# A tanh recurrence on one Trainium2 core: tanh ahead of the transpose, 32-column matmuls, and a bank and a signal for each output half

## The chip, the cores and the metric

The kernel runs on one core of a Trainium2 chip. The metric is the device time of one execution in microseconds (us), lower is better; the median of several runs is compared. Engines are named as in the profile: PE is TensorE's matmul, PEld its weight load, DVE is VectorE, ACT is ScalarE, POOL is GpSimd, SP is SyncE. Each has an instruction stream of its own, and they meet at semaphores.

## The reference

A block with four layers on x (8 batches, 512 positions, 256 channels). Only the first part is touched by the change, a recurrence over the 512 positions whose every step needs the one before:

```python
xw = jnp.einsum('ntd,dh->nth', x, Wx) + b
def step(prev_h, xw_t):
    next_h = jnp.tanh(xw_t + prev_h @ Wh)
    return (next_h, next_h)
_, hs = jax.lax.scan(step, h0, jnp.swapaxes(xw, 0, 1))
```

Its output goes through a long convolution (decays `exp(-dt*A*t)`), is added to x, and a gated scan and a mixture of 16 experts with a shared one follow. Nothing after the recurrence can begin before its last step.

## The kernel before, in words

Everything is written out by hand, engine by engine, with semaphores; nothing reorders it. Constants: B=8 batches, C=2 halves of the 256 channels, Q=32, J=4, W=D/J=64, G=8 steps to a group, IT=32 iterations of 2G=16 steps.

The state h of a step lies in `hring[:, slot, k]`, for each half k a 128 x 8 tile (channels by batches), in a ring of 16 slots. A step on PE is this (`steps`, L535): for each half k it waits for h of the last step (`s_h`, L539) and issues J=4 matmuls (L541), with h as the 8 stationary columns and 64 columns of `wh` moving, one for each quarter j of the output. The four write to partitions 32j to 32j+8 of one PSUM bank (`tile_position`). After the eighth matmul `s_sum` rises by one. The sum in PSUM thus has batches on the partitions and 64 output channels a quarter. Fp32 matmuls appear twice in the trace, so eight of the program are 16 rows of PE and 16 of PEld.

DVE (`turn`, L1060) waits for `s_sum` and makes two 32 x 32 block transposes, one for each half, from PSUM to `zt`, each with a signal `s_zt`. ACT (`steps`, L817) takes tanh of the 8 useful columns of each transposed half (L823), writes it to `hring`, and signals `s_h`. So the loop is matmuls, transpose, tanh, matmuls.

While DVE and ACT are at it, PE has other work, in program order behind the step's own matmuls: `xpart` (L517), the product x Wx and the bias for a step 8 steps ahead, put into the other group's banks (8 matmuls with `wx`, 4 with `brow`), and then `keep_up` (L504), one bf16 matmul of 256 columns on zeros. In 4 of the 16 steps of the first 16 iterations four matmuls of `kernel_sums` (L511) stand in its place. Ahead of the recurrence, `xpart` is made for the first 8 steps.

The loops: PE runs iterations 0 to 15 in one `Fori` (L559), 16 to 30 in a second (L562), each with a body of 16 written-out steps, and the last iteration is written out apart, with no `xpart` in its last 8 steps and 512 columns of `keep_up` instead. POOL copies finished groups of 8 states from `hring` to `big` (`keep`, L359) and signals `s_hist`; ACT waits for it before it writes a ring slot again.

Of the kernel before, what the change touches and what calls it, by code (L numbers as in the profile page):

```python
# [9 lines left out]
ACT = mybir.ActivationFunctionType  # L10
# [3 lines left out]
P = 128  # L14
B, S, D = 8, 512, 256
C = D // P
TB = S // P
R = B * TB
Q = 32
J = P // Q  # L20
W = D // J
FILL = 256
G = 8
# [26 lines left out]
def build(nc, x_tok, x_steps, h0_rec, h0_gate, wx_d, wh_d, b_rec_d, a_bc_d, a_q_d, dt_bc_d, dt_q_d, c_q_d, d_k_d,  # L50
# [6 lines left out]
    with ExitStack() as ctx:  # L57
        def sb(name, shape, dt=F32):
            return ctx.enter_context(nc.sbuf_tensor(name, shape, dt))
# [6 lines left out]
        brow = sb("brow", [1, D])  # L66
        h0r = sb("h0r", [P, C, B])
# [15 lines left out]
        tri = sb("tri", [P, 2, P])  # L83
# [7 lines left out]

        xst = sb("xst", [P, 2, C, G, B])
        zt = sb("zt", [P, 2, W])
        hring = sb("hring", [P, 2 * G, C, B])

        shared = ExitStack()
        wx = shared.enter_context(nc.sbuf_tensor("wx", [P, C, D], F32))
        wh = shared.enter_context(nc.sbuf_tensor("wh", [P, C, D], F32))
# [7 lines left out]
        mid = shared.enter_context(nc.sbuf_tensor("mid", [P, R * D], F32))  # L107
        x1T = mid[:, :].rearrange("p (c r t) -> p c r t", c=C, t=P)
        blank = mid[:, 0:CT * DX].rearrange("p (t d) -> p t d", t=CT)
        arena = shared.enter_context(nc.sbuf_tensor("arena", [P, 11776], F32))  # L110

        def part(at, shape):
# [85 lines left out]
        ps = ctx.enter_context(nc.psum_tensor("ps", [P, 8, 512], F32))  # L198
# [32 lines left out]
            pair = nf if nf < 2 else (nf + 1) % 2  # L231
            return pair, 2 + pair

        def sums_at(group, t):

            return ps[:, 2 * group + t % 2, t // 2 * W:(t // 2 + 1) * W]

        def u_out(engine, copy, half, done):

# [100 lines left out]
        def _(pool):  # L340
# [17 lines left out]

            def keep(i, half):  # L359

                group = hring[:, G * half:G * half + G][:, ::-1].rearrange("p t k b -> p k t b")
                pool.wait_ge(s_zero, 1)
                pool.wait_ge(s_h, 4 * G * i + 2 * G * half + 2 * G + 2)
                pool.tensor_tensor(uT[:, :, bass.ds(i * (-2 * G) + (S - G - G * half), G), :], group, zeros, ALU.add).then_inc(s_hist, 1)  # L364
# [132 lines left out]
        def _(pe):  # L497
# [4 lines left out]
            def keep_up(columns):  # L502

                nc.tensor.matmul(ps[:, 6, 0:columns], zero16[:, 0:P], zero16[:, 0:columns], start=True, stop=True)  # L504

            def kernel_sums(piece):

                half, h = piece // NH, piece % NH
                at = slice(half * P // 2, (half + 1) * P // 2)
                for j in range(CG):  # L510
                    last = nc.tensor.matmul(ps[Q * j:Q * j + J, 4, at], cblk[:, j, h], qx[:, 0, NH * j + h, at], start=piece == 0, stop=h == NH - 1,  # L511
                                            skip_group_check=True, tile_position=(0, Q * j))
                if piece == 2 * NH - 1:
                    last.then_inc(s_kmm, 1)

            def xpart(bank, t):  # L517

                for k in range(C):
                    for j in range(J):  # L520
                        nc.tensor.matmul(sums_at(bank, t)[Q * j:Q * j + B], xst[:, bank, k, t], wx[:, k, j * W:(j + 1) * W],  # L521
                                         start=t < 2 and k == 0, stop=False, skip_group_check=True, tile_position=(0, Q * j))
                for j in range(J):
                    last = nc.tensor.matmul(sums_at(bank, t)[Q * j:Q * j + B], tri[0:1, 1, 0:B], brow[:, j * W:(j + 1) * W],  # L524
                                            start=False, stop=False, skip_group_check=True, tile_position=(0, Q * j))
                return last
            for _ in range(WARM):
                keep_up(512)
# [2 lines left out]
            for t in range(G):  # L531
                last = xpart(0, t)
            last.then_inc(s_xdone, 1)

            def steps(i, bank, more, kernel):  # L535
                for t in range(G):
                    n = bank * G + t
                    for k in range(C):
                        pe.wait_ge(s_h, 4 * G * i + 2 * n + k + 1)  # L539
                        for j in range(J):  # L540
                            last = nc.tensor.matmul(sums_at(bank, t)[Q * j:Q * j + B], hring[:, (n - 1) % (2 * G), k], wh[:, k, j * W:(j + 1) * W],  # L541
                                                    start=False, stop=True, skip_group_check=True, tile_position=(0, Q * j))
                    last.then_inc(s_sum, 1)
                    if more:
                        if t == 0:
                            pe.wait_ge(s_xs[1 - bank], 16 * i + 16 + 16 * bank)
                        last = xpart(1 - bank, t)
                        if t == G - 1:
                            last.then_inc(s_xdone, 1)
                    if kernel and 11 <= n < 11 + 2 * NH:  # L550
                        if n == 11:
                            pe.wait_ge(s_ps0, 1)
                            pe.wait_ge(s_kqe, i + 1)
                            pe.wait_ge(s_kc, i + 1)
                        kernel_sums(n - 11)
                        continue
                    keep_up(FILL if more else 512)
# [13 lines left out]
            n = 0  # L571
            for tb in range(TB):
                for k in range(C):
                    for bq in range(2):
                        if n >= 4:
                            pe.wait_ge((s_uev, s_uea)[n % 2], (n - 4) // 2 + 1)
                        for b in range(4):
                            last = nc.tensor.transpose(ps[:, 2 + n % 4, b * P:(b + 1) * P], uT[:, k, S - (tb + 1) * P:S - tb * P, 4 * bq + b], ident[:])
# [82 lines left out]
            for b in range(B):  # L661
# [3 lines left out]
                for z in range(2):  # L665
# [4 lines left out]
                    for q in range(3):  # L670
                        for c in range(C):
                            last = nc.tensor.matmul(ps[:, 3 * z + q, :], gw[:, q, c, z * P:(z + 1) * P], x1T[:, c, 4 * b:4 * b + 4, :].rearrange("p r t -> p (r t)"), start=c == 0, stop=c == C - 1)  # L672
# [39 lines left out]
            def logits(b):  # L712

                for c in range(C):
                    last = nc.tensor.matmul(ps[Q * (b % J):Q * (b % J) + NE, 4 + b // J, :].rearrange("p (r t) -> p r t", r=TB), rw[:, c], hidT[:, c, 4 * b:4 * b + 4, :],
                                            start=c == 0, stop=c == C - 1, tile_position=(0, Q * (b % J)))
                return last
# [4 lines left out]
            for b in range(B - 2, B):  # L722
                last = logits(b)
# [3 lines left out]
            for q in range(2):  # L727
                for tb in range(TB):
                    last = nc.tensor.transpose(ps[:, 2 * q, tb * P:(tb + 1) * P], lgT[:, q, tb * P:(tb + 1) * P], ident[:])
# [25 lines left out]
            for b in range(B):  # L755
# [3 lines left out]
                if b == 1:  # L759
                    pe.wait_ge(s_cnt, 1)  # L760
                    pe.wait_ge(s_hev, 2 * B)
                    for h in range(2):
                        last = nc.tensor.matmul(ps[:, 6 + h, :], tri[:, h], rt[:, 9], start=True, stop=True)
# [43 lines left out]
        def _(act):  # L807
# [8 lines left out]

            def steps(i, kernel, conv=False):  # L817
                for n in range(2 * G):
                    if n % G == 0:
                        act.wait_ge(s_hist, 2 * i + n // G + 1)  # L820
                    for k in range(C):
                        act.wait_ge(s_zt, 4 * G * i + 2 * n + k + 1)
                        nc.scalar.activation(hring[:, n, k], zt[:, n % 2, k * Q:k * Q + B], ACT.Tanh).then_inc(s_h, 1)  # L823
                    if kernel and 2 <= n < 2 + CG * NH:
                        if n == 2:
                            act.wait_ge(s_kq, i + 1)
                        last = nc.scalar.activation(qx[:, 0, n - 2], qx[:, 0, n - 2], ACT.Exp, scale=-1.0)
                        if n == 1 + CG * NH:
                            last.then_inc(s_kqe, 1)
                    if conv:  # L830
                        first_args(n)
# [197 lines left out]
        def _(dve):  # L1029
# [8 lines left out]
            nc.vector.memset(ps[:, 0:5], 0.0).then_inc(s_ps0, 1)  # L1038
            nc.vector.memset(xc[:], 0.0).then_inc(s_hist, 2)
            dve.wait_ge(s_first, FIRST_LOADED)  # L1040
            nc.vector.tensor_copy(hring[:, 2 * G - 1], h0r[:]).then_inc(s_h, 2)
            dve.wait_ge(s_const, LOADED)
            dve.wait_ge(s_dtm, 4)
            nc.vector.tensor_tensor(dta_q[:], dt_q[:].unsqueeze(2).to_broadcast([P, NG, NH]), a_q[:].unsqueeze(1).to_broadcast([P, NG, NH]), ALU.mult).then_inc(s_dta, 1)
# [13 lines left out]
            IT = S // G // 2  # L1058

            def turn(i, n):  # L1060
                dve.wait_ge(s_sum, 2 * G * i + n + 1)
                bank, t = n // G, n % G
                for k in range(C):
                    nc.vector.transpose(zt[:, n % 2, k * Q:(k + 1) * Q], sums_at(bank, t)[:, k * Q:(k + 1) * Q]).then_inc(s_zt, 1)  # L1064
            def steps(i, kernel):
                for n in range(2 * G):
                    turn(i, n)
                    if kernel and n == 4:
                        kernel_states(i)
                    if kernel and n == 15:  # L1070
                        kernel_out(i)
# [109 lines left out]
            for q in range(2):  # L1181
                for tb in range(TB):
                    last = nc.vector.tensor_tensor(v(0).rearrange("p (b t) e -> p b t e", t=TB)[:, J * q:J * q + J, tb], ps[:, 2 * q, tb * P:(tb + 1) * P].rearrange("p (j e) -> p j e", j=J)[:, :, 0:NE],
                                                   rb[:].unsqueeze(1).to_broadcast([P, J, NE]), ALU.add)
# [7 lines left out]
            for k in range(K):  # L1192
                p, val, at, eq, oh = 2 + 4 * k, 3 + k, 5 + k, 3, 4 + k
# [179 lines left out]
```

## Time and profile before

| | |
|---|---|
| time, median of 3 runs | 1414.28 us (1414.25 to 1425.42) |
| span of the profiled execution | 1422.2 us |
| recurrence in it, from the first L541 matmul to the last | 12.1 to about 555.6 us |
| one step in it, at the full granted clock | about 1.00 us |
| PE / PEld / DVE / ACT / POOL busy | 84% / 61% / 49% / 36% / 36% of the span |

How to read the rows: a timeline row gives the start and the duration of a run of like instructions on one engine, then line, operation, output and inputs, shapes and their number, and in brackets how long the engine sat idle before it and what ended that.
### The profile page before, as it was taken

Reading aid. Unit: us, or ns where it says so; the run is one execution under the profiler, and the core shown is the slowest. Engines: PE = TensorE matmul, PEld = TensorE weight load, DVE = VectorE, ACT = ScalarE, POOL = GpSimd, SP = SyncE. Lnnn points to the kernel's source line nnn. Section 1 sums busy time; section 2 is a strip of 40 time slices with the busy share of each in tenths; the row PEclk is TensorE's granted clock in tenths of the full one; section 3 lists DMA queues with packets and bytes.
Section 4 is the critical chain, followed back from the end, with each engine's and each line's share of the span. In section 5 each row is a group of like instructions: output and inputs, shape, how many; then the busy total and the mean of one; then the engine's idle time right before and its main releaser. Section 6 shows DMA issues by size and latency. Waiting matters only on the chain.

```text
span 1422.2 us, 62375 instructions
## 1 busy us (share of the span) xinstructions
PE 1191.2 (84%) x26162; PEld 864.1 (61%) x26180; DVE 694.7 (49%) x1803; ACT 491.8 (35%) x1775; POOL 512.9 (36%) x390
## 2 busy tenths in 40 slices
PE   7999999989999997898964753799498898988970
PEld 4666666656666665454432331477498898988970
DVE  2333333313333333455599997855254545545437
ACT  2444434313333335343322221223144444444430
POOL 1111121300000000454377777577544444444430
PEclk9999999969999997999987876899798988989985
DMA  1111111124330012686000000032222232323109
GB/s 43 53 39 39 37 38 54 39 84 137 113 111 9 7 47 55 136 164 115 32 1 0 0 0 0 1 127 81 81 102 83 100 127 79 119 68 114 65 27 352
DMA packets 89028, 102.45 MB, mean 72 GB/s; under 512 B 9967, under 2 KB 70534, under 8 KB 88978
## 3 DMA queue, kind: packets, MB, share of 16 engines
q1 hardware_dynamic: 82066, 88.62, 21.3%
q0 software_dynamic: 6912, 13.14, 2.7%
q8 instruction: 35, 0.57, 0.2%
q14 instruction: 15, 0.12, 0.0%
HBM read 65.23 MB, written 42.28 MB: 76 GB/s over the span
## 4 chain that ended last, share of the span: by engine, by line
PE 59%; DVE 16%; issue 10%; DMA 5%; POOL 5%; ACT 3%; SPq 2%; DVEq 0%; POOLq 0%; ACTq 0%
PE ps L541 13%; PE ps L782 10%; PE ps L521 8%; PE ps L524 8%; PE ps L504 8%; PE ps L793 6%; DVE eact_lo L1266 5%; DMA arena<-k_pad 4%; POOL slots_in L464 4%; DVE arena L1145 2%; DVE arena L1137 2%; DVE arena L1143 1%; PE ps L592 1%; DVE arena L1132 1%; SPq L293 1%
## 5 line engine op out<-in xcount | busy, mean ns | idle before, releaser
L1064 DVE STREAM_TRANSPOSE zt<-ps 128x32 f32<-128x32 f32 x1024 | 160.6, 195 | 378.6 <-PE ps L541 378.6
L823 ACT ACTIVATE hring<-zt 128x8 f32<-128x8 f32 x1024 | 158.5, 201 | 355.7 <-DVE zt L1064 355.5
L541 PE MATMUL ps<-wh,hring 128*8 128x64 f32 x8192 | 217.1, 224 | 10.3 <-issue 8.0
L521 PE MATMUL ps<-wx,xst 128*8 128x64 f32 x8192 | 214.2, 222 | 6.7 <-issue 6.5
L504 PE MATMUL ps<-zero 128*128 128x256 bf16 (+2 forms) x582 | 163.0, 283 | 3.6 <-DVE ps L1038 3.6
L364 POOL TENSOR_TENSOR big<-hring,zero 128x128 f32 (+1 forms) x64 | 29.1, 454 | 378.1 <-ACT hring L823 378.1
L541 PEld LDWEIGHTS ps<-wh,hring 128*8 128x8 f32 x8192 | 120.1, 88 | 74.5 <-issue 12.5
L524 PE MATMUL ps<-brow,tri 1*8 1x64 f32 x4096 | 152.0, 218 | 0.0
L521 PEld LDWEIGHTS ps<-wx,xst 128*8 128x8 f32 x8192 | 143.6, 91 | 9.9 <-issue 9.0
L793 PE MATMUL ps<-ew_hi,eact_hi 128*128 128x256 f32 (+1 forms) x240 | 87.3, 364 | 42.3 <-ACT arena L976 42.3
L782 PE MATMUL ps<-xgT_hi,ew_hi 128*128 128x320 f32 (+1 forms) x384 | 118.7, 309 | 0.9 <-DVE xgT_lo L1256 0.9
L782 PE MATMUL ps<-xgT_lo,ew_hi 128*128 128x320 f32 (+1 forms) x384 | 118.3, 308 | 0.0
L782 PE MATMUL ps<-xgT_hi,ew_lo 128*128 128x320 f32 (+1 forms) x384 | 118.1, 307 | 0.0
L348 POOL TENSOR_TENSOR arena<-dta_q,iota_t 128x1024 f32<-128x1024 f32 x32 | 60.7, 1898 | 156.0 <-PE ps L511 101.5
L487 POOL DMA_INDIRECT results<-arena,dest x80 | 78.7, 984 | 103.2 <-ACT arena L976 73.9
L473 POOL TENSOR_TENSOR ew_lo<-arena,ew_hi 128x2176 fp32r<-128x2176 f32 x16 | 77.9, 4868 | 104.0 <-issue 86.0
L504 PEld LDWEIGHTS ps<-zero 128*128 128x128 bf16 x600 | 57.8, 97 | 91.5 <-issue 40.4
L1272 DVE TENSOR_TENSOR mid<-mid,ps 128x320 f32<-128x320 f32 (+1 forms) x96 | 46.7, 486 | 136.3 <-ACT mid L982 134.7
L1266 DVE TENSOR_TENSOR eact_lo<-mid,eact_hi 128x320 fp32r<-128x320 f32 (+1 forms) x96 | 103.4, 1077 | 2.1
L524 PEld LDWEIGHTS ps<-brow,tri 1*8 1x8 f32 x4096 | 57.2, 82 | 58.9 <-issue 3.6
L672 PE MATMUL ps<-mid,gw 128*128 128x512 f32 x192 | 87.5, 612 | 0.8 <-ACT mid L888 0.8
L793 PEld LDWEIGHTS ps<-ew_hi,eact_hi 128*128 128x128 f32 (+1 forms) x240 | 59.8, 249 | 45.4 <-ACT arena L976 36.1
(156 smaller groups left out, 2142.4 us busy)
## 6 DMA issues: line engine op xcount, KB each, us to landing
arena<-k_pad SPq DMA_DIRECT2D x64, 256.0 KB, 6.7
slots_in<-mid SPq DMA_DIRECT2D x16, 642.5 KB, 6.4
mid<-slots_in SPq DMA_DIRECT2D x16, 642.5 KB, 4.3
results<-zero SPq DMA_DIRECT2D x16, 512.0 KB, 3.2
arena<-in_ex_down SPq DMA_DIRECT2D x16, 384.0 KB, 5.6
arena<-in_ex_gate SPq DMA_DIRECT2D x16, 352.0 KB, 4.6
arena<-in_ex_up SPq DMA_DIRECT2D x16, 352.0 KB, 5.2
xst<-in_x_steps SPq DMA_DIRECT2D x64, 64.0 KB, 1.8
```

Of the source, the lines that this page charges most:

```text
L473: pool.tensor_tensor(ew_lo[z][:], ew[:, z], ew_hi[:, z].bitcast(F32), ALU.subtract).then_inc(s_wlo, 1)
L487: pool.indirect_dma_start(out=results[:, :], out_offset=bass.IndirectOffsetOnAxis(ap=dest[:, z, t:t + 1], axis=0), in_=yo[:, z, t], in_off ...
L504: nc.tensor.matmul(ps[:, 6, 0:columns], zero16[:, 0:P], zero16[:, 0:columns], start=True, stop=True)
L521: nc.tensor.matmul(sums_at(bank, t)[Q * j:Q * j + B], xst[:, bank, k, t], wx[:, k, j * W:(j + 1) * W], start=t < 2 and k == 0, stop=False, ...
L524: last = nc.tensor.matmul(sums_at(bank, t)[Q * j:Q * j + B], tri[0:1, 1, 0:B], brow[:, j * W:(j + 1) * W], start=False, stop=False, skip_g ...
L541: last = nc.tensor.matmul(sums_at(bank, t)[Q * j:Q * j + B], hring[:, (n - 1) % (2 * G), k], wh[:, k, j * W:(j + 1) * W], start=False, sto ...
L672: last = nc.tensor.matmul(ps[:, 3 * z + q, :], gw[:, q, c, z * P:(z + 1) * P], x1T[:, c, 4 * b:4 * b + 4, :].rearrange("p r t -> p (r t)") ...
L782: last = nc.tensor.matmul(ps[0:fw, 2 * h + m % 2, 0:HALF], of(w)[:, c, f0:f0 + fw], v[:, c, hf * HALF:(hf + 1) * HALF], start=c == 0 and p ...
L793: last = nc.tensor.matmul(ps[:, 4 + (z + t) % 2, 0:D], a[0:fw, f, t * P:(t + 1) * P], down_of(w)[0:fw, f], start=f == 0 and p == 0, stop=f ...
L823: nc.scalar.activation(hring[:, n, k], zt[:, n % 2, k * Q:k * Q + B], ACT.Tanh).then_inc(s_h, 1)
L1064: nc.vector.transpose(zt[:, n % 2, k * Q:(k + 1) * Q], sums_at(bank, t)[:, k * Q:(k + 1) * Q]).then_inc(s_zt, 1)
L1266: nc.vector.tensor_tensor(eact_lo[0:fw, f, at], eprod[0:fw, m % 2], eact_hi[0:fw, f, at].bitcast(F32), ALU.subtract).then_inc(s_elo, 1)
```

## The change

- PE: every matmul of the recurrence that wrote 64 columns becomes two that write 32 each, in `xpart` (L521, L524) and in the step (L541). `sums_at` now takes the output half: half 0 of all 8 steps of a group lies in one bank, half 1 in another. `s_sum` rises twice a step, once for each half, when the matmuls of k=1 for this half are done. Ahead of the second half's matmuls of k=0 PE waits for `s_zt`, that is for both tanh of the last step.
- ACT: tanh comes first, straight from PSUM, on 128 x 32, into `zt`; it waits for `s_sum` and signals `s_zt`.
- DVE: each transpose now comes after, from `zt` to `hring`, waits for `s_zt` and signals `s_h`; the wait for `s_hist` moves from ACT to DVE.
- `hring` has 32 columns a slot instead of 8, and moves to a free part of `mid`; PE, POOL and the first copy of h read or write its first 8 columns.

```diff
-        def sums_at(group, t):
-
-            return ps[:, 2 * group + t % 2, t // 2 * W:(t // 2 + 1) * W]
+        def sums_at(group, t, half):
+
+            return ps[:, 2 * group + half, t * Q:(t + 1) * Q]
...
                 for k in range(C):
+                    for m in range(C):
+                        for j in range(J):
+                            nc.tensor.matmul(sums_at(bank, t, m)[Q * j:Q * j + B], xst[:, bank, k, t], wx[:, k, j * W + m * Q:j * W + (m + 1) * Q],
+                                             start=t == 0 and k == 0, stop=False, skip_group_check=True, tile_position=(0, Q * j))
+                for m in range(C):
                     for j in range(J):
-                        nc.tensor.matmul(sums_at(bank, t)[Q * j:Q * j + B], xst[:, bank, k, t], wx[:, k, j * W:(j + 1) * W],
-                                         start=t < 2 and k == 0, stop=False, skip_group_check=True, tile_position=(0, Q * j))
-                for j in range(J):
-                    last = nc.tensor.matmul(sums_at(bank, t)[Q * j:Q * j + B], tri[0:1, 1, 0:B], brow[:, j * W:(j + 1) * W],
-                                            start=False, stop=False, skip_group_check=True, tile_position=(0, Q * j))
+                        last = nc.tensor.matmul(sums_at(bank, t, m)[Q * j:Q * j + B], tri[0:1, 1, 0:B], brow[:, j * W + m * Q:j * W + (m + 1) * Q],
+                                                start=False, stop=False, skip_group_check=True, tile_position=(0, Q * j))
                 return last
...
                         pe.wait_ge(s_h, 4 * G * i + 2 * n + k + 1)
-                        for j in range(J):
-                            last = nc.tensor.matmul(sums_at(bank, t)[Q * j:Q * j + B], hring[:, (n - 1) % (2 * G), k], wh[:, k, j * W:(j + 1) * W],
-                                                    start=False, stop=True, skip_group_check=True, tile_position=(0, Q * j))
-                    last.then_inc(s_sum, 1)
+                        for m in range(C):
+                            for j in range(J):
+                                last = nc.tensor.matmul(sums_at(bank, t, m)[Q * j:Q * j + B], hring[:, (n - 1) % (2 * G), k, 0:B], wh[:, k, j * W + m * Q:j * W + (m + 1) * Q],
+                                                        start=False, stop=True, skip_group_check=True, tile_position=(0, Q * j))
+                            if k == 0 and m == 0 and n >= 1:
+                                pe.wait_ge(s_zt, 4 * G * i + 2 * n)
+                            if k == 1:
+                                last.then_inc(s_sum, 1)
...
                 for n in range(2 * G):
-                    if n % G == 0:
-                        act.wait_ge(s_hist, 2 * i + n // G + 1)
                     for k in range(C):
-                        act.wait_ge(s_zt, 4 * G * i + 2 * n + k + 1)
-                        nc.scalar.activation(hring[:, n, k], zt[:, n % 2, k * Q:k * Q + B], ACT.Tanh).then_inc(s_h, 1)
+                        act.wait_ge(s_sum, 4 * G * i + 2 * n + k + 1)
+                        nc.scalar.activation(zt[:, n % 2, k * Q:(k + 1) * Q], sums_at(n // G, n % G, k), ACT.Tanh).then_inc(s_zt, 1)
...
-                dve.wait_ge(s_sum, 2 * G * i + n + 1)
-                bank, t = n // G, n % G
+                if n % G == 0:
+                    dve.wait_ge(s_hist, 2 * i + n // G + 1)
                 for k in range(C):
-                    nc.vector.transpose(zt[:, n % 2, k * Q:(k + 1) * Q], sums_at(bank, t)[:, k * Q:(k + 1) * Q]).then_inc(s_zt, 1)
+                    dve.wait_ge(s_zt, 4 * G * i + 2 * n + k + 1)
+                    nc.vector.transpose(hring[:, n, k], zt[:, n % 2, k * Q:(k + 1) * Q]).then_inc(s_h, 1)
```

How the program of PE stands, at the start of the first loop (L559 before, L565 after), its first step and the start of the second. The number behind x is that of the program's matmuls; 8x64 means 8 stationary and 64 moving columns. Before:

```order
L559 UNCONDITIONAL_BRANCH
L559 ISA
L541 MATMUL ps<-wh,hring 8x64 x4
L539 REGISTER_ALU
L541 MATMUL ps<-wh,hring 8x64 x4
L546 ISA
L521 MATMUL ps<-wx,xst 8x64 x8
L524 MATMUL ps<-brow,tri 8x64 x4
L504 MATMUL ps<-zero 128x256
L539 REGISTER_ALU
```

And after (`hring` now goes by the name of the tensor that holds it, `mid`):

```order
L544 MATMUL ps<-wh,mid 8x32 x8
L522 MATMUL ps<-wx,xst 8x32 x16
L526 MATMUL ps<-brow,tri 8x32 x8
L504 MATMUL ps<-zero 128x256
L541 REGISTER_ALU
L544 MATMUL ps<-wh,mid 8x32 x8
L541 REGISTER_ALU
```

A step is 20 fp32 matmuls and one bf16 before, and 40 and one after. The order of the kinds of work is unchanged.

ACT in the loop, first before and then after: the operation reads `zt` before and `ps` after, and it is 32 columns wide instead of 8.

```order
L823 ACTIVATE hring<-zt 128x8
L822 REGISTER_ALU
L823 ACTIVATE hring<-zt 128x8
L822 REGISTER_ALU
L823 ACTIVATE hring<-zt 128x8
```

```order
L827 ACTIVATE zt<-ps 128x32
L826 REGISTER_ALU
L827 ACTIVATE zt<-ps 128x32
L826 REGISTER_ALU
L827 ACTIVATE zt<-ps 128x32
```

The number of operations on ACT and of transposes on DVE stays at two a step; each transpose now has a wait of its own ahead of it.

## Rows read from the trace of the kernel before

**Rows 1.** The page: span, and PE's busy time, share, instructions.

```profile
span 1422.2 us, 62375 instructions
PE 1191.2 (84%) x26162; PEld 864.1 (61%) x26180; DVE 694.7 (49%) x1803; ACT 491.8 (35%) x1775; POOL 512.9 (36%) x390
```

**Rows 2.** Timeline, one step at the full clock: start, duration, engine, instructions.

```profile
400.63 0.41 PE L541 MATMUL ps<-wh,hring 128*8 128x64 f32 x16
400.86 0.41 PE L521 MATMUL ps<-wx,xst 128*8 128x64 f32 x16
401.11 0.31 DVE L1064 STREAM_TRANSPOSE zt<-ps 128x32 f32<-128x32 f32 x2 [0.69 <-PE ps L541]
401.19 0.29 PE L524 MATMUL ps<-brow,tri 1*8 1x64 f32 x8
401.36 0.31 ACT L823 ACTIVATE hring<-zt 128x8 f32<-128x8 f32 x2 [0.70 <-DVE zt L1064]
401.42 0.28 PE L504 MATMUL ps<-zero 128*128 128x256 bf16 x1
401.63 0.24 PE L541 MATMUL ps<-wh,hring 128*8 128x64 f32 x3
```

**Rows 3.** Timeline of PE in the first loop's first iteration, with two stalls.

```profile
15.72 0.29 PE L521 MATMUL ps<-wx,xst 128*8 128x64 f32 x6
16.54 0.38 PE L521 MATMUL ps<-wx,xst 128*8 128x64 f32 x10 [0.53 <-issue]
16.85 0.29 PE L524 MATMUL ps<-brow,tri 1*8 1x64 f32 x8
17.08 0.28 PE L504 MATMUL ps<-zero 128*128 128x256 bf16 x1
...
19.30 0.41 PE L541 MATMUL ps<-wh,hring 128*8 128x64 f32 x16
19.52 0.29 PE L521 MATMUL ps<-wx,xst 128*8 128x64 f32 x8
20.61 0.30 PE L521 MATMUL ps<-wx,xst 128*8 128x64 f32 x8 [0.79 <-issue]
```

**Rows 4.** DMA queues in 9 to 33 us: packets, MB, share.

```profile
q8 instruction: 6, 0.10, 1.7%
```

**Rows 5.** DMA queues in 33 to 270 us, all that are listed.

```profile
q1 hardware_dynamic: 8880, 9.96, 12.7%
q14 instruction: 1, 0.01, 0.0%
```

**Rows 6.** DMA queues in 270 to 305 us, and in 530 to 556 us.

```profile
q8 instruction: 6, 0.10, 1.0%
...
q8 instruction: 4, 0.07, 0.9%
```

**Rows 7.** DMA queue q8: the whole span, and the 0.1 us from 17.85.

```profile
q8 instruction: 35, 0.57, 0.2%
...
q8 instruction: 1, 0.02, 73.2%
```

**Rows 8.** Timeline of PE in the second loop's first iteration: the rows with stalls.

```profile
277.45 0.41 PE L541 MATMUL ps<-wh,hring 128*8 128x64 f32 x15 [0.56 <-issue]
...
282.24 0.41 PE L541 MATMUL ps<-wh,hring 128*8 128x64 f32 x13 [1.50 <-issue]
...
286.49 0.41 PE L541 MATMUL ps<-wh,hring 128*8 128x64 f32 x11 [0.95 <-issue]
```

**Rows 9.** Timeline of PE: start of the recurrence, and its last steps.

```profile
12.07 0.41 PE L541 MATMUL ps<-wh,hring 128*8 128x64 f32 x16
...
552.01 0.61 PE L541 MATMUL ps<-wh,hring 128*8 128x64 f32 x16
553.20 0.61 PE L541 MATMUL ps<-wh,hring 128*8 128x64 f32 x16
554.39 0.61 PE L541 MATMUL ps<-wh,hring 128*8 128x64 f32 x16 [0.58 <-ACT hring L823]
```

**Rows 10.** Timeline rows of ACT (near 60 us) and POOL (near 302 us) in the recurrence.

```profile
60.16 0.29 ACT L827 ACTIVATE arena<-arena 128x128 f32<-128x128 f32 x1
...
301.93 0.46 POOL L364 TENSOR_TENSOR big<-hring,zero 128x128 f32 x1 [15.99 <-ACT hring L823]
```

More of the change, by code:

```diff
@@ L93, in build @@
         zt = sb("zt", [P, 2, W])
-        hring = sb("hring", [P, 2 * G, C, B])
         shared = ExitStack()
@@ L109, in build @@
         blank = mid[:, 0:CT * DX].rearrange("p (t d) -> p t d", t=CT)
+        hring = mid[:, 4096:4096 + 2 * G * C * Q].rearrange("p (n k q) -> p n k q", n=2 * G, k=C)
         arena = shared.enter_context(nc.sbuf_tensor("arena", [P, 11776], F32))
@@ L359, in keep @@
             def keep(i, half):
-                group = hring[:, G * half:G * half + G][:, ::-1].rearrange("p t k b -> p k t b")
+                group = hring[:, G * half:G * half + G, :, 0:B][:, ::-1].rearrange("p t k b -> p k t b")
                 pool.wait_ge(s_zero, 1)
@@ L1040, in _ @@
             dve.wait_ge(s_first, FIRST_LOADED)
-            nc.vector.tensor_copy(hring[:, 2 * G - 1], h0r[:]).then_inc(s_h, 2)
+            nc.vector.tensor_copy(hring[:, 2 * G - 1, :, 0:B], h0r[:]).then_inc(s_h, 2)
             dve.wait_ge(s_const, LOADED)
```

## The prediction

> **What bounds the kernel now.** First the page: PE is busy 84% of the span and far ahead of every other engine [rows 1], so the first question is whether the recurrence waits for the loop matmuls, transpose, tanh, or for PE's own queue. The timeline of one step answers it. PE's starts follow each other without a hole: the step's own matmuls 0.23 us, wx 0.33, brow 0.23, keep_up 0.21, together 1.00 us [rows 2]. The loop through the other engines takes almost the same: the matmuls end at 401.04, DVE starts at 401.11, ACT at 401.36, and the next matmuls at 401.63, just after the first tanh can have ended (401.36 plus about 0.2) [rows 2]. So the two are balanced at 1.00 us, and 512 steps with their stalls fill 12.07 to about 555.6 us (last matmuls at 554.39 plus one step of 1.2) [rows 9].
>
> Then look for stretches in which this doesn't hold. In the first iteration of the first loop PE stops with the word "issue", in the middle of a run of wx matmuls, where nothing in the program waits: it resumes at 16.54 and again at 20.61 us [rows 3]. The DMA queues say what it is: queue q8, "instruction", moves six packets while the loop is run for the first time [rows 4], none in its 15 further iterations [rows 5], six again at the first pass of the second loop, and four at the last iteration [rows 6]. PE's program comes in pieces. Their size: between the two resumptions lie 10+8+1 matmuls, two whole steps of 41 (in the lines left out) and 16+8, that is 125 [rows 3]; each has its weight load, and three steps have two register instructions each: 256. A packet is 0.57 MB / 35 = 16.3 KB [rows 7], so 64 bytes an instruction. Their pace: 20.61 - 16.54 = 4.07 us from piece to piece, though the instructions in it take only 3.1 us; at the second loop 4.79 and 4.25 us, with 1.50 and 0.95 us of idle time [rows 8]. The next packet starts at 17.9, 1.35 us after the resumption, and its instructions run 2.7 us after that [rows 7, 3].
>
> **The change part by part.** *The loop between the engines.* Half 0 is handed on a quarter of the step's matmuls earlier. The half-0 loop is then three quarters of them plus the latency, 0.41 - 0.06 = 0.35 us, plus the unchanged 0.07 + 0.25 + 0.27 between the starts of DVE, ACT and PE [rows 2]: 0.94 instead of 1.00. That gain is real only if PE can use it. Tanh grows from 8 to 32 columns and reads PSUM; the trace has no such operation. Between the present 0.2 and the 0.29 us of a 128-column activation [rows 2, 10] I take 0.2. The transposes keep their shape. POOL's copy out of wider slots takes 0.46 us once in 8 steps after 16 us of idleness [rows 10], so neither it nor the moved wait for it costs anything; without that cover DVE's transposes would stand behind the wait and PE behind them, 0.46 us a group at most. The new wait for s_zt asks for tanh that the transposes ahead of s_h have needed already, but for the second half's, done by then: nothing.
>
> *PE's time in a step.* 40 matmul rows of the trace become 80, with half the columns. Now 16 take 0.23 us, 14 ns each [rows 2]. Between pace by columns (7 ns: no change, 1.00 us a step) and pace by instruction (14 ns: 40 more rows, +0.56 us) nothing in the trace decides; for the forecast below either is hidden.
>
> *PE's program.* This is the term that decides. A step is 20 fp32 matmuls of four instructions (two matmuls, two weight loads) plus two: 82; 40 give 162. The first loop's body is 16 x 82, plus 56 (four steps have 16 instructions for two) and 32 of registers: 1400, 5.5 pieces; it becomes 2680, 10.5 pieces. The second goes from 5.25 to 10.25. Five and a half pieces stay on the chip from iteration to iteration [rows 5]. Whether ten and a half do, no row shows: the bounds are all kept (no refetch) and none kept. I take none, because the store is evidently filled on demand and in order, and a body that outgrows such a store has overwritten its head when it branches back; I see no reason why it should be twice as large as what it holds today.
>
> By the Trainium skill (Runtime: NRT & Kernel Launch, Instruction fetch mechanics) PE's instruction memory is a FIFO of 128 KiB, 2048 instructions, refilled in blocks of 256. The block agrees with the 256 counted here; the capacity no row here shows. It lies between 1400 and 2680, and by it the sum is the one below. The same section says that a branch outside a window of two pages forces a fetch, and this trace disagrees: 5.5 pieces, 15 branches back, no packet.
>
> *The sum, none kept.* A piece holds 256/162 = 1.6 steps, 1.6 to 2.5 us of work, less than 4.07, so pieces set the pace. The body touches 11 pieces: ten arrivals at 4.07 (41), about 1 us in the last, partly filled one, and 4.0 for the head after the branch: 45 us an iteration (rounded down), where it is 16 now. 31 iterations: 1395 us. Ahead of them xpart has 784 instructions instead of 400: one more piece to wait for, start at 16.5 instead of 12.1. The last iteration: five pieces (20.5 us), then 8 steps without xpart at about 1.19 us (553.20 to 554.39 [rows 9]), 30 us. End of the recurrence: 16.5 + 1395 + 30 = 1441; now 555.6; difference +886. Everything after is untouched. Against the profiled span 1422.2 + 886 = 2308; the median of the runs lies 8 us below that span: **2300 us**.
>
> Bounds of this case. Low: if the next packet is asked for by the number of instructions run and not after a time, the 1.35 us become 0.7 and the piece 3.4 us; with no surcharge at the branch 10.4 x 3.4 x 31 = 1096, plus 43: 1997 us. High: the 4.79 us of rows 8 for each of 11 pieces plus 1 us, 31 times, 1668 + 50: 2576 us.
>
> **The rivals.**
> *Part of the body survives* (the store is not overwritten in order): say 6 of 11 pieces refetched, 6 x 4.07 + 5 x 1.6 = 32 us an iteration, about 1910 us. Against it speaks only that in-order filling fits all rows.
> *All of it stays, step at 1.00 us.* Then only first passes cost: some 27 pieces of the longer program at 4.07 - 1.6 = 2.5 us of stall, 68, less the present 13: 1414 + 55 = 1469 us. For it: the store holds 5.5 pieces, and its end is not seen.
> *All of it stays, pace by instruction.* +0.56 us x 512 = 287, and 27 x 1.6 - 13 = 30 for first passes: 1731 us. The trace has no shorter matmul to decide it. By the Trainium skill (TensorE: Matmul & The Clock Gate, Back-to-back issue gap) matmuls of 1 to 64 columns all take about 25 ns; a program matmul takes 28 here, so rule and row are near, and the rule would give 20 x 25 ns, some 1700 us by an estimate from it.
> *No difference.* All stays and pieces come ahead of need: 1414 us. By the Trainium skill (the Runtime section above) crossing a block boundary is mostly hidden; that would be this case. The rows disagree: 0.53 to 1.50 us of idleness at every first crossing read here.
> *Faster.* The other side, by one mechanism: the half-0 loop of 0.94 us sets the step. 0.06 x 512 = 31 us: 1383. It decides only if stalls vanish (55 us eat it) and PE's own 1.00 us, which has no hole today, falls too, below 0.97.
>
> **How the numbers follow.** None kept 0.70; partly kept 0.06; kept and paced by instruction 0.08; kept and 1.00 us a step 0.10; no difference 0.03; faster 0.03. A measurement here can tell about 1%. Faster 0.03, same 0.03, slower 0.94. The first case alone spans 1997 to 2576. For eight in ten the range needs the 1731 and 1910 too: 1700 to 2580; left out are 1469, the last two cases, and the outer edge of the first.
>
> **What would show it.** Right: q8 moves packets through the whole recurrence, some 31 x 11 + 30, about 370 instead of 35; PE idles on "issue" by 1.5 to 2.5 us every 125 matmuls; the recurrence ends near 1440 us; DVE and ACT wait for PE; the last kernel_sums and the convolution look as before. The granted clock may fall to half for want of work, which costs nothing while pieces set the pace. Wrong: no q8 packets in the later iterations; then the step's length (1.0 or 1.56 us) tells the two kept cases apart. If q8 is busy but pieces come every 3 us or less, the pace was mis-sized, and if only some return, the fill order was.

## The result, and the profile after

The changed kernel takes 2367.18 us (median of 4 runs, 2365.28 to 2372.9), the kernel before 1419.62 us beside it: 1.666 times as long, 95% interval 1.659 to 1.673. The kernel before had median times between 1420 us (here) and 1469 us in the comparisons below, so each ratio is against runs of it in the same comparison; in one of them (the first with keep_up left out) 7 of its 13 runs were in a slower state, near 1556 us, and the ratios there go by the other six, 1420 to 1439 us.

The page of the profile after: span, busy times, granted clock and the instruction queue.

```profile
span 2371.0 us, 103846 instructions
PE 1568.3 (66%) x46641; PEld 1160.9 (49%) x46660; DVE 702.9 (30%) x1803; ACT 492.1 (21%) x1775; POOL 511.6 (22%) x390
PEclk6555555555555555555555555799877997889886
q8 instruction: 398, 6.52, 1.2%
```

PE has 20,500 more matmuls than in [rows 1] and is busy for a smaller share. Queue q8 moved 398 packets instead of 35 [rows 7]. The clock is at half for the whole recurrence, some 25 of the 40 slices.

The waits of PE between 16.8 and 1508 us (us in total, times, longest), and the packets of q8 in that stretch:

```profile
PE ps L544 <- issue: 322.7, 170, 3.7
PE ps L522 <- issue: 155.2, 96, 5.0
PE ps L526 <- issue: 107.4, 93, 1.5
PE ps L544 <- DVE mid L1069: 2.1, 5, 0.5
```

```profile
q8 instruction: 377, 6.18, 1.8%
```

359 stops on "issue", 585 us, against 2.1 us of waiting for DVE: the loop through tanh and transpose, which the change is about, is no longer what PE waits for. Such stops stand in the middle of a run of matmuls, as in [rows 3]; the third and the fourth row below are the starts of a step without one and of the next:

```profile
701.50 0.55 PE L544 MATMUL ps<-wh,mid 128*8 128x32 f32 x27 [2.13 <-issue]
...
705.11 0.40 PE L522 MATMUL ps<-wx,xst 128*8 128x32 f32 x16 [1.17 <-issue]
...
706.09 0.62 PE L544 MATMUL ps<-wh,mid 128*8 128x32 f32 x32
...
707.72 0.39 PE L544 MATMUL ps<-wh,mid 128*8 128x32 f32 x13
709.70 0.51 PE L544 MATMUL ps<-wh,mid 128*8 128x32 f32 x19 [1.59 <-issue]
```

A step without a stop takes 1.63 us at the half clock (706.09 to 707.72), so 512 of them would be about 835 us by an estimate from it. The recurrence took 1491 us: the lower clock alone does not make this time.

The recurrence begins with the first of these rows; the second is the first matmul behind it, which stood at 556.32 us before:

```profile
16.85 0.61 PE L544 MATMUL ps<-wh,mid 128*8 128x32 f32 x32
...
1507.76 0.49 PE L584 MATMUL ps<-ident,big 128*128 128x128 f32 x2 [0.94 <-POOL big L364]
```

From that matmul to the end it is 2371.0 - 1507.8 = 863 us, before 1422.2 - 556.3 = 866. All of the difference lies in the recurrence.

### The profile page after: what moved, and what is told of

It reads as the page before. It is cut to its first block, busy times and chain, and to the rows that moved or that the text cites. A ratio compares the mean times of both kernels' runs of the same rounds, so it can differ in the third digit from the quotient of the medians.

```text
span 2371.0 us, 103846 instructions
## 1 busy us (share of the span) xinstructions
PE 1568.3 (66%) x46641; PEld 1160.9 (49%) x46660; DVE 702.9 (30%) x1803; ACT 492.1 (21%) x1775; POOL 511.6 (22%) x390
## 4 chain that ended last, share of the span: by engine, by line
PE 52%; issue 30%; DVE 10%; POOL 3%; DMA 3%; ACT 2%; SPq 1%; DVEq 0%; POOLq 0%; ACTq 0%
PE ps L544 13%; PE ps L522 10%; PE ps L526 8%; PE ps L504 7%; PE ps L788 6%; PE ps L799 4%; DVE eact_lo L1271 3%; POOL slots_in L464 2%; DMA arena<-k_pad 2%; DVE arena L1150 1%; DVE xtok L1300 1%; DVE arena L1142 1%; PE ps L598 1%; PE ps L511 1%; DVE arena L1148 1%
## 5 line engine op out<-in xcount | busy, mean ns | idle before, releaser
L544 PE MATMUL ps<-wh,mid 128*8 128x32 f32 x16384 | 353.2, 239 | 324.8 <-issue 322.7
L1069 DVE STREAM_TRANSPOSE mid<-zt 128x32 f32<-128x32 f32 x1024 | 167.6, 198 | 1321.5 <-ACT zt L827 1321.5
L544 PEld LDWEIGHTS ps<-wh,mid 128*8 128x8 f32 x16384 | 246.7, 110 | 450.1 <-issue 446.6
L522 PE MATMUL ps<-wx,xst 128*8 128x32 f32 x16384 | 349.0, 241 | 158.3 <-issue 158.3
L827 ACT ACTIVATE zt<-ps 128x32 f32<-128x32 f32 x1024 | 159.6, 197 | 1305.8 <-PE ps L544 1305.8
L522 PEld LDWEIGHTS ps<-wx,xst 128*8 128x8 f32 x16384 | 268.2, 116 | 176.4 <-issue 175.7
L526 PE MATMUL ps<-brow,tri 1*8 1x32 f32 x8192 | 227.8, 231 | 107.4 <-issue 107.4
L364 POOL TENSOR_TENSOR big<-mid,zero 128x128 f32 (+1 forms) x64 | 28.8, 450 | 1148.6 <-DVE mid L1069 1148.6
L504 PE MATMUL ps<-zero 128*128 128x256 bf16 (+2 forms) x581 | 208.8, 362 | 3.6 <-DVE ps L1042 3.6
L526 PEld LDWEIGHTS ps<-brow,tri 1*8 1x8 f32 x8192 | 122.6, 98 | 176.5 <-issue 123.6
```

Of the source, the lines that this page charges most:

```text
L522: nc.tensor.matmul(sums_at(bank, t, m)[Q * j:Q * j + B], xst[:, bank, k, t], wx[:, k, j * W + m * Q:j * W + (m + 1) * Q], start=t == 0 and ...
L526: last = nc.tensor.matmul(sums_at(bank, t, m)[Q * j:Q * j + B], tri[0:1, 1, 0:B], brow[:, j * W + m * Q:j * W + (m + 1) * Q], start=False, ...
L544: last = nc.tensor.matmul(sums_at(bank, t, m)[Q * j:Q * j + B], hring[:, (n - 1) % (2 * G), k, 0:B], wh[:, k, j * W + m * Q:j * W + (m + 1 ...
L827: nc.scalar.activation(zt[:, n % 2, k * Q:(k + 1) * Q], sums_at(n // G, n % G, k), ACT.Tanh).then_inc(s_zt, 1)
L1069: nc.vector.transpose(hring[:, n, k], zt[:, n % 2, k * Q:(k + 1) * Q]).then_inc(s_h, 1)
```

## The experiments

**Only PE's code made longer.** The kernel before, with two iterations in each pass of PE's loops; every matmul as it was.

```diff
-            with pe.Fori(0, NCH) as i:
-                for bank in range(2):
-                    steps(i, bank, True, True)
+            with pe.Fori(0, NCH // 2) as p:
+                for h in range(2):
+                    for bank in range(2):
+                        steps(2 * p + h, bank, True, True)
```

(and the second loop likewise, with one iteration written out behind it)

> The kernel before with nothing changed but PE's loops: each pass holds two iterations (32 steps) instead of one, so every matmul keeps its shape, its order and its count. The bodies grow to about 2800 and 2690 instructions, 10.9 and 10.5 pieces of 256. Theory (PE's instruction store overflows and every pass refetches its body, one piece per 4.07 us): a pass takes about 48.5 us instead of 32.1, 15 passes, so about 1414 + 250 = 1660 us, and some 15 x 12 + 20 = 200 packets on q8 instead of 35. Rival (the split matmuls, the new order or the lower clock make the time, the code's length does not): 1414 us within 1%, about 35 packets.

Measured: 1787 us in one run, against 1457 for the kernel before: 1.23 times. Queue q8, in the whole span and in 40 to 885 us:

```profile
q8 instruction: 219, 3.59, 0.9%
...
q8 instruction: 194, 3.18, 1.6%
```

So the length of the code alone brings the refetching, with no split matmul and no new order. The packets came nearly as forecast (219 for 200: mostly 13 a pass in place of 12), the time was higher: +330 us, not +250. A pass of the first loop took 54.7 us instead of 48.5. The granted clock accounts for a part of this. Windows of this run (stretch, length, PE, PEld, DVE, ACT, POOL busy, PEclk, DMA share, GB/s):

```profile
40.00:460.00 420.00, 346.47 (x10670) 217.47 (x10670) 83.83 (x545) 101.80 (x620) 47.54 (x49) 0.70 0.10 32
460.00:885.00 425.00, 348.70 (x9824) 211.82 (x9824) 77.15 (x491) 80.70 (x505) 14.02 (x31) 0.65 0.16 47
```

It was 1.00 in nearly all of the recurrence before. At half clock a step of this kernel takes 1.63 us (the matmuls of a step start at 409.17 and 410.80), so a piece of 3.1 steps is 5.1 us of work, more than the 4 us of its fetching. Then PE has work while the next piece comes, and the clock, not the fetch, sets the pace. The stop below stands behind steps of 1.00 us; but behind the stop that ended at 138.80 us PE ran 849 rows of matmul, 6.8 pieces, up to the branch back without another over 0.3 us, 29.9 us of work, 4.4 us a piece:

```profile
139.00:171.40 32.40, 29.87 (x849) 18.85 (x839) 6.60 (x43) 7.50 (x46) 5.06 (x5) 0.58 0.08 25
```

I had taken the clock to be free here. It is free only where a piece holds less work than its fetch takes. How the 80 us divide between the clock and the thirteenth packet of a pass, this one run does not show.

```profile
408.34 0.29 PE L521 MATMUL ps<-wx,xst 128*8 128x64 f32 x6 [1.26 <-issue]
...
409.17 0.62 PE L541 MATMUL ps<-wh,hring 128*8 128x64 f32 x16
...
410.80 0.62 PE L541 MATMUL ps<-wh,hring 128*8 128x64 f32 x16
```

**The change with a body that fits, and its control.** Groups of 4 steps, so that a body holds 8 steps.

```diff
-G = 8
+G = 4
-PIECES = 8
+PIECES = 16
...
-                    if kernel and 11 <= n < 11 + 2 * NH:
+                    if kernel and n >= 2 * G - 2:
```

(with two kernel_sums and two exponentials a step in fewer steps)

> The changed kernel with groups of 4 steps instead of 8, so that PE's loop bodies hold 8 steps, some 1350 instructions or 5.3 pieces, with the same split matmuls, the same order of tanh and transpose and the same banks and signals. (The decay work of the convolution kernel moves into the first 128 steps, two exponentials a step, and input loads come in pieces half as large; all of the computation is there.) Theory: no packets on q8 but at first passes, the clock goes back to full, and a step takes 1.0 us, so about 1430 us. Rival 1 (a matmul costs its issue, not its columns): 1.56 us a step, about 1730 us. Rival 2 (the split work itself, not the fetching, holds the clock at half): some 1.6 us a step, about 1750 us.

> Control for the run with groups of 4: the kernel before with the same groups of 4 steps and the same shifted side work. Its bodies hold some 700 instructions, 2.8 pieces. Both theories: 1414 us within 1%, perhaps 1400, since fewer pieces are met for the first time in the loops (some 10 instead of 16, each about 1 us of stall).

Measured: the changed kernel 1526.87 us against 1457.38, ratio 1.053 (1.043 to 1.063). The control 1454.7, ratio 0.999 (0.995 to 1.004), so grouping by 4 is neutral. Of the changed kernel so built, q8 in 50 to 610 us, and the windows row of 210 to 610:

```profile
q8 instruction: 5, 0.08, 0.1%
```

```profile
210.00:610.00 400.00, 400.00 (x28786) 313.72 (x28770) 110.41 (x710) 103.19 (x710) 28.44 (x89) 1.00 0.13 40
```

The same split matmuls, order, banks and signals: no refetching, full clock, and 69 us over the kernel before in place of 948. That isolates the cause of nearly all of the loss. Both rivals of this run fall: matmuls are not paced by instruction at 14 ns, and the split work doesn't hold the clock down. But the forecast of 1.00 us a step was wrong too. 710 transposes in 400 us are 1.127 us a step, and PE has no idle time. The timeline of one step:

```profile
302.07 0.42 PE L543 MATMUL ps<-wh,mid 128*8 128x32 f32 x32
302.31 0.51 PE L521 MATMUL ps<-wx,xst 128*8 128x32 f32 x32
302.74 0.30 PE L525 MATMUL ps<-brow,tri 1*8 1x32 f32 x16
302.98 0.28 PE L503 MATMUL ps<-zero 128*128 128x256 bf16 x1
303.19 0.42 PE L543 MATMUL ps<-wh,mid 128*8 128x32 f32 x32
```

From start to start, against [rows 2]: 0.24 (0.23), 0.43 (0.33), 0.24 (0.23), 0.21 (0.21). The step's own 32 matmuls go at 7.5 ns each, half of the 14 ns before: pace by columns. The 32 wx matmuls right behind them take 0.10 us more than 16 wide ones did.

**One part alone: tanh ahead of the transpose.** 64-column matmuls, one s_sum a step, banks as before.

```diff
+                    act.wait_ge(s_sum, 2 * G * i + n + 1)
                     for k in range(C):
-                        act.wait_ge(s_zt, 4 * G * i + 2 * n + k + 1)
-                        nc.scalar.activation(hring[:, n, k], zt[:, n % 2, k * Q:k * Q + B], ACT.Tanh).then_inc(s_h, 1)
+                        nc.scalar.activation(zt[:, n % 2, k * Q:(k + 1) * Q], sums_at(n // G, n % G)[:, k * Q:(k + 1) * Q], ACT.Tanh).then_inc(s_zt, 1)
```

> One part of the change alone: tanh straight from PSUM ahead of the transpose, with the matmuls of 64 columns, one signal for the sums and the banks as before. PE's program is as long as before. Theory: 1414 us within 1%, since PE's own 1.00 us a step stays and the loop through ACT and DVE has the same two operations. Rival (tanh on 128 x 32 from PSUM or transposes one by one cost more than they did): up to 0.1 us a step, 1465 us.

Measured: 1457.1 us, ratio 1.001 (0.997 to 1.006). As expected: the order alone changes nothing, and a step takes 1.000 us (420 transposes in 310 to 520 us), PE's own time as before.

**How much the store holds.** The changed kernel (groups of 8), with bias and part of x Wx left out to shorten the bodies.

```diff
-                for k in range(C):
+                last = None
+                for k in range(0 if t not in (3, 6) else C, C):
...
-                for m in range(C):
-                    for j in range(J):
-                        last = nc.tensor.matmul(sums_at(bank, t, m)[Q * j:Q * j + B], tri[0:1, 1, 0:B], brow[:, j * W + m * Q:j * W + (m + 1) * Q],
-                                                start=False, stop=False, skip_group_check=True, tile_position=(0, Q * j))
```

> The changed kernel with part of the work left out, to find where the instruction store ends: the bias matmuls are left out of every step, and x Wx out of 4 of the 16 steps of a body. The bodies are 1912 and 1856 instructions long, 7.5 and 7.25 pieces, and touch 8 pieces each, where the kernel before touches 7 and the changed one 11. If the store holds 8 pieces and needs none of them for the piece fetched ahead: no q8 packets after first passes, about 50 in all, steps of 0.9 to 1.0 us, about 1400 us. If the piece fetched ahead takes the place of the oldest, so that 8 are one too many, or if the store is smaller: all are fetched again, 8 x 4.07 + 4 = 36 us an iteration, 31 times, about 290 packets and 2000 us.

Measured: 1983 us, one run. q8 in 40 to 1055 us:

```profile
q8 instruction: 260, 4.26, 1.8%
```

That is the second of the two outcomes, with its numbers (2000 us, about 290 packets; the whole span had 302). A body of 7.5 pieces is already too long.

How many pieces a body touches can be read from the trace, since PE stops where a piece ends. Between the stops of a pass of the first loop it runs 21 rows of matmul, seven times 124 to 127, and 40: nine pieces, not the eight that I had counted, and nine packets. In the second loop it runs 84, six times 125 or 126, and 74: eight pieces, and nine packets, one of them fetched ahead and not used. So it is the second loop that shows eight to be too many.

The same kernel with still less, the bias left out and x Wx out of 8 of the 16 steps:

> The run before this one with still less: the bias left out of every step, and x Wx out of 8 of the 16 steps of a body. The bodies are 1656 and 1600 instructions, 6.5 and 6.25 pieces, and touch 7 pieces each, as many as in the kernel before. Theory (8 pieces are held, of which one is the piece fetched ahead, so 7 can be kept): no q8 packets but at first passes, about 40 in all, steps of about 0.95 us, about 1400 us. Rival (what grows with the split matmuls, not the count of pieces, makes PE fetch again): 7 x 4.07 + 4 = 32 us an iteration, about 260 packets, 1900 us.

Measured: 1552 us, one run, 92 packets. In the first loop, 49.8 to 266.9 us, q8 doesn't appear among the queues: 6.5 pieces that touch 7 are kept. The second loop did what neither side expected. Of its later iterations six took 31 to 35 us with nine packets each and the others about 16 us with none, in turn until the last two; two neighbours, 293.0 to 309.8 (no row for q8) and 309.8 to 343.5:

```profile
q8 instruction: 9, 0.15, 2.3%
```

In a refetched pass PE runs 21 rows of matmul, six pieces, and 11: eight pieces, the last of which holds only some 22 instructions. A body that touches 7 pieces was kept (first loop here, 6.5 long, and in the kernel before, 5.5 long); one that touches 8 was refetched whole where 74 rows lie in the last piece (second loop of the run before), and in every other pass where 11 do. A piece fetched ahead near the end of the body, which takes the place of the first one, fits both; that it is this is not shown.

**Without keep_up.** In the changed kernel with groups of 4, in the one with the new order alone, and in the kernel before:

```diff
-                    keep_up(FILL if more else 512)
+                    if not more:
+                        keep_up(512)
```

> The changed kernel with groups of 4 steps, without the keep_up matmul in the steps that have x Wx. With it a step takes 1.117 us there, and PE's own work sets it (0.27 + 0.41 + 0.23 + 0.21), while the loop through ACT and DVE needs 0.94. Theory: without keep_up the loop sets the step, 0.94 to 0.95 us, so 0.17 x 512 = 87 us less than with it, about 1440 us, 1% under the kernel before on the same chip (1457). Rival (keep_up is what keeps the clock at full): the clock falls to half and a step takes 1.3 us or more, 1600 us or more.

> Tanh ahead of the transpose alone (64-column matmuls, one signal), without keep_up in the steps that have x Wx. With it the steps take 1.003 us, the ones in which kernel_sums stand in its place 0.973. Theory: PE no longer sets the step, the loop does: 0.973 us, 15 us less than with it, about 1% under the kernel before. Rival (the clock falls without keep_up): over 1500 us.

> Control: the kernel before without keep_up in the steps that have x Wx. The steps in which kernel_sums stand in its place take 0.989 us, the others 1.002. Theory: 0.989 us a step, 7 us less, within 1% of the kernel before. Rival (the clock falls without keep_up): over 1500 us.

Measured, in this order: 1432.76 us and ratio 1.003 (0.998 to 1.007); 1397.45 us and 0.978 (0.960 to 0.996); 1407.12 us and 0.985 (0.968 to 1.002), which leaves open whether the last gained anything. The windows rows for DVE (length, busy, number of transposes, clock, DMA share, GB/s), in this order:

```profile
200.00:550.00 350.00, 109.48 (x704) 1.00 0.14 45
```

```profile
300.00:510.00 210.00, 67.18 (x432) 1.00 0.24 76
```

```profile
310.00:520.00 210.00, 66.74 (x425) 1.00 0.23 72
```

Two transposes a step: 0.994, 0.972 and 0.988 us a step, all at full clock. The rival of all three, that keep_up holds the clock, falls: at 1.00 in these stretches it is not needed. The steps of the second and the third kernel came out as expected, those of the first did not (0.994 instead of 0.94). Its rows:

```profile
300.02 0.49 PE L543 MATMUL ps<-wh,mid 128*8 128x32 f32 x32
300.32 0.49 PE L521 MATMUL ps<-wx,xst 128*8 128x32 f32 x32
300.74 0.30 PE L525 MATMUL ps<-brow,tri 1*8 1x32 f32 x16
300.75 0.31 DVE L1072 STREAM_TRANSPOSE mid<-zt 128x32 f32<-128x32 f32 x2 [0.68 <-ACT zt L828]
301.01 0.42 PE L543 MATMUL ps<-wh,mid 128*8 128x32 f32 x32
...
302.17 0.47 PE L543 MATMUL ps<-wh,mid 128*8 128x32 f32 x32 [0.19 <-DVE mid L1072]
```

The steps fall into two kinds. Of 351 steps between 200 and 550 us, 308 take 0.97 us, and 43 take 1.16 us; in each of these 43, such as the one from 301.01 to 302.17, PE's loop branches back, which a body of 8 steps does twice as often as one of 16. In the short ones PE is behind brow at once, and also 0.26 us behind the first transpose (300.75 to 301.01), as early as in any step of this trace: PE's own work and the loop end together.

The kernel with the new order and no keep_up was run again, with eleven more runs of the kernel before beside it.

> Tanh ahead of the transpose alone, without keep_up in the steps that have x Wx, once more against the kernel before, since that kernel's own times lay far apart in the last comparison. Theory: steps of 0.973 instead of 1.002 us, 15 us, and shorter stretches at half clock behind the first passes: about 0.985 of the kernel before. Rival (the gain was the other kernel's disturbed times): 1.00.

Measured: 1447.31 us against 1469.49, ratio 0.985 (0.980 to 0.990). It beats both kernels, by 1.5% over the one before. Not all of this is the order's: in the comparison above it was 0.7% under the kernel before without keep_up (1397.45 to 1407.12 us, no run of either among the other's), 10 us, near the 8 us that 512 steps of 0.972 instead of 0.988 us make. Now PE waits for DVE in each step, so the loop through the engines sets the time:

```profile
301.16 0.31 DVE L1064 STREAM_TRANSPOSE mid<-zt 128x32 f32<-128x32 f32 x2 [0.66 <-ACT zt L822]
301.43 0.23 PEld L541 LDWEIGHTS ps<-wh,mid 128*8 128x8 f32 x16 [0.30 <-DVE mid L1064]
```

## Why the prediction was right, point by point

*What decides* was right, and shown: the code's length alone brings the refetching (1787 us, 219 packets), and with a short body it is gone (5 packets, full clock). The forecast was 2300 us, measured 2367.

*None of the body is kept*: 12 packets came in every iteration, where the sum had 11 pieces. Between the stops of the first loop PE runs 84 rows of matmul, nine times 126 or 127, and 103: eleven pieces, and the twelfth packet, 1.4 us behind another, is fetched ahead of the branch back and not used. In the second loop it runs 21, ten times 126 or 127, and 11: twelve pieces, and none to spare. Three stretches of whole iterations in the changed kernel, 193.5 to 739.4 us (12 iterations), 836.5 to 1189.2 (7) and 1189.2 to 1426 (5):

```profile
q8 instruction: 144, 2.36, 1.9%
```

```profile
q8 instruction: 84, 1.38, 1.6%
```

```profile
q8 instruction: 60, 0.98, 1.8%
```

About 370 packets were forecast for the recurrence, 377 came. That they agree so well is luck: 31 x 11 + 30 was forecast, and about 31 x 12 + 5 came.

*Where the 67 us came from.* The term of the sum that was mis-sized is the 45 us an iteration in the second loop. The first loop: 545.9 / 12 = 45.5 us, against 45; its packets are 4.00 us apart but for the one at 1.4, so the pace of 4.07 from [rows 3] held. The second loop took 740.0 us for its fifteen (739.4 to 1479.4 us, from branch to branch), where the prediction had 15 x 45 = 675: +65 of the +66 by which the recurrence was too short (1490.9 measured, 1424.5 predicted).

Two things were missing. The body touches twelve pieces there, as said: in the quiet stretch an iteration takes 236.8 / 5 = 47.4 us, twelve times 3.95. And an iteration of the stretch from 836.5 to 1189.2 us takes 352.7 / 7 = 50.4 us. Six times in it two packets stand 6.3 to 7.7 us apart, the others 3.99 on the mean; this makes 18 of the 21 us by which it is longer than seven quiet iterations. Just then the input rows x_tok and the zeroing of slots_in are on the DMA queues, as in 911.0 to 918.6 us, between two packets of q8:

```profile
q1 hardware_dynamic: 515, 1.67, 69.0%
```

Each of the six gaps has at least 375 packets of q1. That these delay the instructions is likely; no run leaves them out. [Rows 8] had shown 4.79 and 4.25 at the start of the second loop, and I used them for the bound only and the first loop's 4.07 for both.

*Start and end*: 16.85 us (16.5 predicted), the last iteration 28.4 us (30), and the rest of the program unchanged, 863 against 866 us.

*The clock*: it fell to half, as the prediction allowed for, at no visible cost there, since the pieces of the first loop came every 4.00 us at half clock, as fast as the 4.07 us of [rows 3] at full. A piece is 1.6 steps, 2.6 us of work at 1.63 us a step. In the run with only longer code, where a piece holds twice the work, the same fall is part of the 80 us by which I was off. "Costs nothing" holds for one of the two.

*The rivals.* All kept with 1.00 us a step, and all kept with pace by instruction, both had the step wrong: it is 1.12 us, between their 1.00 and 1.56. Partly kept doesn't occur for this kernel, but does occur in the border case above. The faster rival was right on its loop, but just: in the run without keep_up ACT starts 0.45 us after the matmuls at the earliest, DVE 0.23 after that and PE 0.27 after that, 0.95, near the predicted 0.94. At the median of 189 steps ACT starts after 0.47 us, since the step's own matmuls then take 0.30 instead of 0.24 us, and the step is 0.97 us. So handing half 0 on early gained nothing over the new order alone, 0.97 us too. With keep_up the loop never decides, since the split raised PE's own time at once. So even with code that fits, the change as made costs 5.3%; what can be had from it is the order of tanh and transpose, once keep_up is gone, and that is worth about 0.7%.

*The rule of the Trainium skill on the instruction memory* (Runtime: NRT & Kernel Launch, Instruction fetch mechanics) gives PE 128 KiB in blocks of 16 KiB, that is 8 blocks. The runs agree, with one addition they show: a body that touches 7 blocks was kept in every pass, bodies that touch 8 were not, which fits the block fetched ahead taking a place. *The rule on small matmuls* (TensorE: Matmul & The Clock Gate, Back-to-back issue gap) gives about 25 ns for 1 to 64 columns. By an estimate from it the 16 own matmuls of the program would take 0.40 us a step, and they take 0.24 in the changed kernel with groups of 4.

## What to carry to other kernels

Count the instructions of a loop's body on each engine, as the trace counts them (an fp32 matmul is four), before splitting an operation in it, and where its ends lie: in these runs PE kept a body that touched 7 pieces of 256, and fetched one that touched 9, 11 or 12 whole in each pass, at about 4 us a piece. With 8 it did so in each pass or in every other. The sign in the profile is packets of queue q8 behind the first pass, and PE idle on "issue" within runs of like instructions. And before shortening a loop through several engines, look whether the engine with the filler work starts back to back; here a matmul meant to keep the clock held the step at 1.00 us, 1.2% above what it took without it (0.988), and the clock stayed at full.

## What the hardware showed that I had not expected

The wx matmuls of 32 columns go slower than the same shape just before them: 0.24 us for the step's own 32, 0.43 for the next 32, where the wide ones had 0.33 for 16. Both go at half the former columns and from the same kind of operands. The first can have been brought up while keep_up ran ahead of them (0.21 us), the second not, so instructions may come no faster than about one in 5 ns (64 in 0.32 us, when 0.11 of the 0.43 is the switch to brow, as in [rows 2], where 16 rows at 14 ns take 0.33). The run without keep_up points the same way: nothing keeps PE busy ahead of the step's own 32 there, and they take 0.30 us (300.02 to 300.32). No run here separates that from another cause.

A body that touches eight pieces, the last with 11 rows of matmul, was refetched in every second pass, and not in every or in none.
